# Cross-attention and a top-1 mixture of experts: routed experts on full 256-token tiles of one expert, queued in DRAM

## The reference, cut to what matters

```python
# x, ctx: (16, 256, 256) float32, 16 batches of 256 tokens; out: the same shape
x = x + xattn(layernorm(x), ctx, ctx, Wq, Wk, Wv, Wo)
x = x + ffn(layernorm(x))

def xattn(query, key, value, ...):        # 16 heads of 16, blocks of 64 keys and 64 queries
    ...
    scores = einsum('bhpqd,bhpkd->bhpqk', qg, kg) * scale      # one pair (row block, column block) at a time
    attn = softmax(scores, axis=-1)                            # over the 64 keys of one block
    ob = einsum('bhpqk,bhpkd->bhpqd', attn, vg)
    acc = segment_sum(ob.transpose(2, 0, 1, 3, 4), rows, num_segments=nb)
    ...
    return out @ Wo.T

def ffn(x):                               # D 256, HIDDEN 1024, 2 routed experts and a shared one
    top1 = argmax(softmax(xf @ gate_w.T), axis=-1)
    masked = xf[None] * one_hot(top1, 2).T[:, :, None]
    h = relu(einsum('end,edh->enh', masked, w1) + b1[:, None, :])
    routing_output = (einsum('enh,ehd->end', h, w2) + b2[:, None, :]).sum(axis=0)
    shared = relu(xf @ sw1 + sb1) @ sw2 + sb2
    return routing_output + shared
```

## Time and profile before

| what | us |
|---|---|
| median of 3 runs (lowest, highest) | 1027.59 (1027.53, 1027.85) |
| the profiled execution, its own time | 1027.41 |
| its span in the trace | 1025.4 |
| PE busy | 963.7 (94%) |
| VectorE (DVE) busy | 640.8 (62%) |
| ScalarE (ACT) busy | 528.5 (52%) |
| POOL busy | 458.1 (45%) |
| mean granted TensorE clock | 0.968 |

### The profile page before, as it was taken

One profiled execution on the slowest core, in us unless ns is written; L12 is line 12 of the kernel. 1 busy time (PEld: TensorE's weight loads), 2 busy tenths in 40 slices (PEclk: granted clock), 3 DMA queues, 4 the chain that ended last, 5 costly groups with the idle time before them and its releaser, 6 DMA issues.

```text
span 1025.4 us, 24708 instructions
## 1 busy us (share of the span) xinstructions
PE 963.7 (94%) x9120; PEld 818.7 (80%) x9120; DVE 640.8 (62%) x1073; ACT 528.5 (52%) x1197; POOL 458.1 (45%) x559
## 2 busy tenths in 40 slices
PE   3365999999999999999999999999999999999998
PEld 2245889798888979798897979888797988879688
DVE  4574576765657667565767766675776666576640
ACT  3253555546555554645555464555546454554544
POOL 4353526162453626244362624436272542626254
PEclk8586999999999999999999999999999999999999
DMA  8555250432526043261614226251412526240000
GB/s 252 134 134 92 63 84 21 86 58 61 92 61 82 28 85 51 61 92 61 82 45 76 42 67 87 61 82 61 68 38 73 78 61 88 65 61 17 17 11 12
DMA packets 70885, 71.51 MB, mean 70 GB/s; under 512 B 6224, under 2 KB 68432, under 8 KB 70608
## 3 DMA queue, kind: packets, MB, share of 16 engines
q1 hardware_dynamic: 68944, 64.93, 33.0%
q0 software_dynamic: 1920, 6.29, 2.3%
...
## 4 chain that ended last, share of the span: by engine, by line
PE 90%; DMA 4%; DVE 3%; POOL 1%; ACT 1%; SPq 1%; issue 0%; DVEq 0%; ACTq 0%; POOLq 0%
PE hid L351 29%; PE acc L510 27%; PE nd L434 12%; PE work L351 6%; PE work L418 5%; PE work L399 3%; PE nd L399 2%; PE work L462 2%; PE work L448 1%; DMA h<-w 1%; DMA QP<-scratch_q 1%; DVE nmax L759 1%; PE work L359 1%; PE work L472 1%; DMA QP<-scratch_m 1%; DMA scratch_m<-mT 1%
## 5 line engine op out<-in xcount | busy, mean ns | idle before, releaser
L918 POOL TENSOR_TENSOR hl<-h,hh 128x256 fp32r<-128x256 f32 x384 | 285.0, 751 | 501.4 <-ACT hh L643 501.2
L643 ACT ACTIVATE h<-hid,bias 128x256 f32<-128x256 f32 x384 | 182.4, 475 | 297.6 <-PE hid L351 296.4
L351 PE MATMUL hid<-X,w_hi 128*128 128x256 f32 x1536 | 296.8, 291 | 0.7 <-DVE X L714 0.7
L766 DVE RECIPROCAL T<-nd 128x256 f32<-128x256 f32 x128 | 224.6, 1755 | 98.5 <-PE nd L434 94.4
L351 PEld LDWEIGHTS hid<-X,w_hi 128*128 128x128 f32 x1536 | 234.9, 189 | 32.3 <-issue 21.5
L351 PE MATMUL hid<-X,w_lo 128*128 128x256 f32 x768 | 216.1, 281 | 0.0
L510 PE MATMUL acc<-w_hi,hh 128*128 128x256 f32 x768 | 199.7, 294 | 0.0
L510 PE MATMUL acc<-w_lo,hh 128*128 128x256 f32 x768 | 188.8, 280 | 0.0
L643 ACT ACTIVATE hh<-hid,bias 128x256 fp32r<-128x256 f32 x384 | 182.8, 476 | 0.0
L632 ACT ACTIVATE PT<-work 128x512 f32<-128x512 f32 x256 | 139.7, 604 | 63.7 <-PE work L418 63.7
L510 PEld LDWEIGHTS acc<-w_hi,hh 128*128 128x128 f32 x768 | 144.4, 188 | 24.1 <-ACT hh L643 17.3
...
## 6 DMA issues: line engine op xcount, KB each, us to landing
...
```

Source lines behind the costliest of these rows:

```text
L351: mm = nc.tensor.matmul(dst, R(s), R(m), start=n == 0, stop=n == len(steps) - 1)
L643: last = nc.scalar.activation(dst, hid[:, u % 2, a, :], ACT.Relu, bias=bias1[:, k:k + 1])
L766: nc.vector.reciprocal(T[:, p, :], nd[:, p % 2, 1, :]).then_inc(sem["inverted"], 1)
L918: nc.gpsimd.tensor_tensor(R(hl[:, u % 2, a]), h32[:, u % 2, a], hh[:, u % 2, a], ALU.subtract).then_inc(sem["hl_done"], 1)
```

## The change

The shared expert still runs batch by batch, 4 units. The routed experts no longer run on a batch. After the gate of batch n, POOL works out for each token its place in one of two queues in DRAM (`place`; the ranks come from three small matmuls, `ranks`), and scatters the normalised tokens into `xq` and the half-finished outputs with their token numbers into `yq` (`queue_x`, `queue_y`: two indirect DMAs each). One iteration later a tile of 256 queued tokens, all of one expert, is loaded and run through that expert alone: 4 units. POOL chooses the expert (`chosen`), SyncE reads the choice into registers and loads that expert's first weights from DRAM (`load_w1`, 4 x 512 KB) into one set of buffers, and PE reads it for the address of the second weights. The result is scattered to the rows of `out` (`send_out`: two indirect DMAs). The constant vector of the other expert and all second biases are a table of two rows (`table`, `level`), made once in iteration 1 and added by two matmuls per tile. After the last batch there are three tiles: the 15th full one and the two partly filled ends of the queues. So there are 16 x 4 units of the shared expert and 17 x 4 of tiles; the counts are fixed in the program and don't depend on the routing.

PE's order is rewritten too: scores come in four visits of two doubles, and there are fewer halves of units between the steps. `xhat` has its own buffer for each norm, `add_bias` and the mask work are gone, `x1` is added when the shared expert is finished (`finish_shared`).

```diff
 SP iteration:
+                if tile:
+                    row = load_tile(i - 1)
                 shift(i)
...
+            def load_tile(n):
+                sp.wait_ge(sem["placed"], n + 1)
+                sp.dma_start(log, chosen[0:1, :]).then_inc(sem["logged"], 16)
+                row = sp.value_load(chosen[0:1, 0:1], min_val=0, max_val=QROWS - TILE)
+                expert = sp.value_load(chosen[0:1, 1:2], min_val=0, max_val=1)
+                for u in range(UNITS):
...
+                    load_w1(W1[:, 1], expert, u)
+                    if u == 0:
+                        sp.wait_ge(sem["x_queued"], 32 * (n + 1))
+                        load_tile_x(n, row)
...
 PE iteration:
-                for step, jobs in enumerate(SCORE_STEPS):
-                    for d in jobs:
-                        scores(i, d)
-                    if step % 2 == 0:
-                        up(step // 2 + 1)
-                    else:
-                        down(step // 2)
+                visit(i, 0)
+                if shared:
+                    shared_up(n, 0)
+                    ranks(n, claim(i, ("rk", 0)))
+                    shared_up(n, 1)
+                visit(i, 1)
+                if shared:
+                    shared_down(n, 0)
+                    shared_up(n, 2)
+                visit(i, 2)
+                if shared:
+                    shared_down(n, 1)
+                    shared_up(n, 3)
+                visit(i, 3)
+                if shared:
+                    shared_down(n, 2)
+                    shared_down(n, 3)
                 maxima(i)
-                down(3)
                 if more:
                     front_xT(i + 1)
-                up(5)
+                    front_project(i + 1, "k", 1, c_hi, c_lo, "c_lo")
+                if tile:
+                    tile_tokens(n, claim(i, ("xr", 0), more))
+                    expert = pe.value_load(chosen[0:1, 1:2], min_val=0, max_val=1)
                 if more:
-                    front_project(i + 1, "k", 1, c_hi, c_lo, "c_lo")
-                    front_project(i + 1, "q", 0, a_hi, a_lo, "xT_lo")
-                down(4)
...
+                    front_project(i + 1, "q", 0, a_hi, a_lo, "xT_lo", tile=tile)
+                if tile:
+                    tile_up(n, 0)
+                    tile_up(n, 1)
+                    tile_down(n, 0, expert)
+                if shared and not tile:
+                    table(0)
+                    table(1)
                 scores_t(i, 0, more)
                 for p in range(PAIRS):
-                    if p in PAIR_UP and (more or p > 0):
-                        up(PAIR_UP[p])
-                    if p in PAIR_DOWN and (more or p > 1):
-                        down(PAIR_DOWN[p])
+                    if tile and p == 2:
+                        tile_down(n, 1, expert)
+                    if tile and p == 5:
+                        tile_up(n, 2)
                     if p + 1 < PAIRS:
                         scores_t(i, p + 1, more)
                     values(i, p)
...
 POOL iteration:
+                if shared:
+                    shared_hidden(n, 0)
+                    place(n, choosing=tile)
+                    queue_x(n)
+                    shared_hidden(n, 1)
...
+                if more:
+                    reciprocal_deviation(i + 1, 0)
+                    context_low(i + 1)
...
+                if shared:
+                    shared_hidden(n, 2)
+                    shared_hidden(n, 3)
+                    queue_y(n)
+                if tile:
+                    for u in range(UNITS - 1):
+                        tile_hidden(n, u)
...
+                if tile:
+                    tile_hidden(n, UNITS - 1)
+                reciprocal_deviation(i, 1)
+                if tile:
+                    send_out(n)
...
+            def send_out(n):
+                pool.wait_ge(sem["r_done"], n)
...
+                for t in range(TT):
+                    rows = yt[:, t, D:D + 1].bitcast(I32)
+                    pool.indirect_dma_start(out=out_rows, out_offset=bass.IndirectOffsetOnAxis(ap=rows, axis=0),
+                                            in_=yt[:, t, 0:D], in_offset=None, **partly) \
+                        .then_inc(sem["out_done"], 16)
```

871 lines of the change are left out of this document (598 added, 273 removed).

## The result

| | before | after |
|---|---|---|
| median (lowest, highest), us | 1027.72 (1027.53, 1028.0) | 1105.83 (1104.13, 1107.37) |
| ratio, 95% interval | | 1.0759 (1.0741 to 1.0778) |
| span of the profiled execution | 1025.4 | 1105.1 |
| mean granted TensorE clock | 0.968 | 0.909 |
| end of the last division, iterations 1, 14, 15 | 144.57, 916.32, 974.08 | 148.72, 947.39, 1007.42 |

The changed kernel is 7.6% slower. I had forecast 1014. The page of the changed kernel, beside the earlier trace rows: PE is busy for 863 us instead of 964, yet the span grew by 80. The second row shown is the granted clock in 40 slices (in tenths of full speed), the third the group of matmuls that read `hl`, with 62.9 us of idle time ahead of them, put down to POOL.

The account below looks back on a forecast made before the run. PE bounds the kernel before; afterwards one batch's chain through all engines, with POOL costing 2 us a cycle. Span 149 + 13 x 56.6 + 52.6 + 75 = 1012, plus 2.0 around it: 1014 us, range 1000 to 1028 (8 in 10: 982 to 1058).

Parts of the forecast that it names:

- the cycles: Loop time from one iteration's last division (t) to the next: 56.6 us forecast, 2.8 less than before, 13 of them.
- the 15th: The cycle up to iteration 15's last division, with no next batch to prepare: 52.6 us forecast.
- the tail: From iteration 15's last division to the end, shared units then three tiles: 75 us forecast, against 51.3 before.
- iteration 1: Iteration that makes the table and has no tile: its last division forecast at 149 us instead of 144.6.
- Step 1: From t, the last division, to the next maxima: tokens ready at t + 7.9, maxima starting at t + 11.5.
- Step 2: Maxima and POOL's queue: scatter 1.0, `place` 3.1, `norm1_apply` 0.85; `shared_down` 3 ends at t + 27.2, POOL costing 2 us.
- rival (b): POOL's queue dearer: each 0.1 us on a scatter adds 0.4 a cycle; at 1.6, 1050, at 2.0, 1073; chance 0.22.
- rival (d): If PE's wait in `shared_down` 1 passes 3.27 us, the clock halves: about 2 a cycle, 1042; chance 0.08.
- the rule on shared ports: VectorE and GpSimd (POOL) share SBUF ports under an exclusive lock, so a scatter could stand still during `norm1_stats` or `norm1_apply`.
- Steps 3 and 4: From `shared_down` 3 to transposed scores 9.2 us (t + 36.4), then 3.0 to the first division and 17.2 for eight pairs.
- (a): Scatters as cheap as plain DMA issues, 0.55 us: VectorE's chain sets a cycle of 55.0, total 990; chance 0.22.
- (c): Weight reload or SyncE's register loads delay the `shift` beyond its 2.8 us slack: 1.5 a cycle, 1035; chance 0.08.

Follow-up runs that it names:

- e1: Changed kernel with POOL issuing a tile's `send_out` one iteration later, behind the `hl` of shared unit 3; 1079.88 us, ratio 1.050.
- e8: Changed kernel with the reload of the first weights cut to 128 of 512 KB per load from the second tile on (output wrong); 1101.20 us, ratio 1.072.
- e3: Changed kernel with two extra up halves on PE, results overwritten, between the `hh` and `hl` matmuls of `shared_down` 1; 1093.45 us, ratio 1.064.
- e16: e15 with two moves on POOL: `context_low` behind the `hl` of shared unit 0, the next norm's power ahead of `queue_x`; 1058.99 us, ratio 1.030.
- e15: e1 plus VectorE making shared unit 1's `hl`, `context_low` first on POOL, two of four weight loads ahead of the tokens' load, reordered end; 1043.15 us, ratio 1.014.
- e4: Changed kernel with all six indirect scatters per iteration made direct DMAs to fixed rows (output not the reference's); 1034.43 us, ratio 1.007.
- e14: Changed kernel with the edits of e1 and e4 together (output not the reference's); 1036.26 us, ratio 1.010.
- e5: Changed kernel with only POOL reordered: `context_low` and `hl` of shared units 0 and 1 ahead of `place`, `queue_x` and `send_out` later; 1128.36 us, ratio 1.097.
- e9: e5 with SyncE issuing all four first-weight loads and biases ahead of the tokens' load, and a changed order at the end; 1145.09 us, ratio 1.117.

## Why the prediction was wrong

The forecast of the span was 1012, the span is 1105. The 93 us are 13 x 4.84 = 63 in the cycles, 7.4 in the 15th, 22.7 in the tail; iteration 1 (149 forecast, 148.72) was right, in part by luck: in e1 and e8, which leave that stretch as it is, the mark stands at 146.9.

**Step 1 was right.** Tokens at t + 7.9, maxima from t + 11.5.

**Step 2 failed**, in the sizes of its terms. Where forecast and trace stand, relative to t:

| | forecast | after |
|---|---|---|
| `send_out` done | 13.7 | 14.75 |
| `place` done | 18.2 | 20.2 |
| second pair of scatters | 20.4 | 22.9 |
| `hl` of shared unit 1 | 21.8 | 24.3 |
| last maxima | 26.0 | 31.0 |
| `shared_down` 3 | 27.2 | 31.8 |

A scatter costs 1.46 of POOL's time in its chain (5.8 for four), not 1.0: I had priced the instruction and not the gap and the spacer ahead of it. `place` costs 4.0, not 3.1. My bounds (2.9 to 4.6) held it, but the value that I took was no middle: 8 steps of 0.27 and 9 of 0.1, the least that I allowed, already make 3.1. The 4.0 is read off the row; no run makes `place` cheaper by itself. By my formula for rival (b) the two are 4 x 0.46 + 0.9 = 2.7 a cycle, and the `hl` of unit 1 came 2.5 late.

Then rival (d) came on top: the clock fell in the wait of 3.74 us. It wasn't the 3.27 of my condition that counted, since it fell in e1's wait of 2.60 too. PE lost 2.1 by it, and 56.6 + 2.5 + 2.1 = 61.2, measured 61.4. The closeness flatters the sum, for the two don't simply add: e3 got back 1.3 to 1.6, not 2.1, because VectorE's last maxima, with the `norm1_apply` that took 1.3 longer than I had it, were only 1.1 ahead of PE. I had treated (b) and (d) as alternatives with a chance each, though (d) follows from (b): a longer queue is a longer wait, and in the longer wait the clock fell. One case of both, priced at about 61 a cycle, was the one that came.

**norm1_apply** took 2.11 instead of 0.85, with `context_low` and the next `hl` beside it. I had weighed the rule on shared ports for the scatters, where no row shows it (in e16 a scatter issued beside `norm1_apply` took 1.12, in the changed kernel 1.11 without it), and not for the two engines' ordinary instructions, where they do. The Trainium skill, SBUF — State Buffer, section "Who interferes with whom", says that a VectorE instruction with two SBUF inputs contends with a GpSimd instruction that reads SBUF, that a `tensor_scalar` can do so in a two-port mode, and that `tensor_reduce` on this chip never does. The traces agree: the gate step took 1.50 beside `context_low` and 0.42 without, the apply 2.11 and 1.55 (e15) beside POOL's subtractions and 0.74 (e16) without, and the reductions 1.28 a pair whatever POOL did. In which mode the apply ran no row tells. (The row on which I had weighed the rule was weak: the division stood beside the last 0.2 us of the DMA issue only, 62.43 against 62.11 to 62.66.) In the changed kernel it wasn't on the longest chain, since PE with its lower clock was 1.1 later; in e3 it was.

**Steps 3 and 4 were about right.** From the end of `shared_down` 3 to the transposed scores 8.8 (9.2 forecast), then 2.98 (2.96), then 17.7 for eight divisions (17.2).

**The rivals.** (a) gave 55.0 a cycle with scatters at 0.55; e4 and e14 have about that price and cycles of 57.3, 56.4 where the clock holds. Even these kernels aren't faster than the one before. (c) does not hold for the change as it stands (e8), but became real as soon as the tokens were queued 3 to 4 us later (e5, e9). The slack that I had put at 2.8 was rather 1.5, an estimate from e5: there the transposed scores start 3.6 after the issue of the second half of the bounce, for which they had waited, and in the changed kernel that issue is at t + 35.5 and the transposed scores start at t + 40.6.

**The tail**, 97.7 against 75. The shared units ended at t + 32.9 (31 forecast). The three tiles took 51.6 against 39: PE waited 4.3 for `hl`, which I had in, and 3.4 for `xt` and 2.4 for its rounding, which I had not; and it was busy for 41.8, not 34, some of it at the lower clock. From the last accumulation to the end it took 13.2 instead of 5, of which 7.8 are POOL's DRAIN.
